# Moving the load of a chunk's shifted rows ahead of a store, the transposes ahead of a layer, and spreading the table gathers 12, 12, 12, 3 instead of 10, 10, 10, 9

## What is computed

```python
e = jnp.stack([tbl_0[ids[:, 0]], ..., tbl_38[ids[:, 38]]], axis=1)      # (2048, 39, 16)
x0 = xk = e
for idx, (W, b) in enumerate([(w0, b0), (w1, b1), (w2, b2)]):
    z = jax.nn.relu(jnp.einsum('bhd,bkd,hks->bsd', x0, xk, W) + b[None, :, None])
    if idx != 2:
        xk = z[:, :64, :]; direct.append(z[:, 64:, :])
    else:
        direct.append(z)
z = jnp.sum(jnp.concatenate(direct, axis=1), axis=-1)                   # (2048, 256)
h = jnp.concatenate([z, dense_ctx], axis=1)
y = relu(relu(h @ W_top1 + b_top1) @ W_top2 + b_top2) @ W_top3
```

## Time and profile before

| | |
|---|---|
| median of 3 runs | 2711.19 us |
| the profiled execution, its own time | 2712.57 us |
| its span, first to last instruction | 2710.9 us |
| mean granted TensorE clock | 0.97 |
| busy: PE, DVE | 2447.7 us (90%), 2228.0 us (82%) |
| busy: ACT, POOL | 1502.6 us (55%), 1610.5 us (59%) |
| DMA | 481.11 MB, mean 177 GB/s |

### The profile page before, as it was taken

The page is one execution under the profiler, slowest core; times in us unless marked ns, Lnnn a source line. Parts: engine busy times, 40 slices in busy tenths (PEclk is TensorE's granted clock), DMA queues, the critical chain, the costliest instruction groups (busy, mean ns, idle before and its releaser), DMA issues.

```text
span 2710.9 us, 27181 instructions
## 1 busy us (share of the span) xinstructions
PE 2447.7 (90%) x7840; PEld 1481.2 (55%) x7840; DVE 2228.0 (82%) x1358; ACT 1502.6 (55%) x1798; POOL 1610.5 (59%) x1093
## 2 busy tenths in 40 slices
PE   0689989898998989999898998989899898989999
PEld 0356555555565555556555555655566555556653
DVE  0679979797998979799798988979789798989970
ACT  0456556565665655556565555655566565556652
POOL 6456657566665756666665666666576566634440
PEclk9899999999999999999999999999999999999999
DMA  2977687777768877776877777787777787787720
GB/s 82 227 184 206 159 195 209 151 201 179 195 168 204 211 146 201 178 181 180 210 188 170 194 176 178 193 203 178 175 199 173 176 205 186 173 186 208 203 67 0
DMA packets 267897, 481.11 MB, mean 177 GB/s; under 512 B 20075, under 2 KB 42715, under 8 KB 267797
## 3 DMA queue, kind: packets, MB, share of 16 engines
q1 hardware_dynamic: 146950, 275.14, 42.0%
q10 hardware_dynamic: 100480, 200.29, 28.3%
q0 software_dynamic: 20448, 5.45, 1.5%
HBM read 470.96 MB, written 9.84 MB: 177 GB/s over the span
## 4 chain that ended last, share of the span: by engine, by line
PE 38%; DVE 18%; issue 17%; DMA 11%; ACT 6%; POOL 4%; SPq 3%; another core or an unknown queue 2%; ACTq 1%; DVEq 0%; POOLq 0%
PE z L796 19%; PE z L775 17%; DVE prod L479 14%; DMA x_diag<-x_transposed 10%; DVE lo_parts L251 3%; ACT hi_parts L610 2%; POOL lo_parts L251 2%; POOL emb L409 1%; ACT hi_copy L624 1%; SPq L300 1%; PE z L897 1%; DVE logit L520 1%; SPq L301 1%; PE xk L897 1%
## 5 line engine op out<-in xcount | busy, mean ns | idle before, releaser
L479 DVE TENSOR_TENSOR prod<-x_pairs,xk 128x2048 f32<-128x2048 f32 x640 | 1432.6, 2280 | 68.5 <-PE z L796 44.7
L251 POOL TENSOR_TENSOR lo_parts<-prod,hi_parts 128x1024 fp32r<-128x1024 f32 x384 | 916.5, 2387 | 759.4 <-ACT hi_parts L610 736.5
L775 PE MATMUL z<-prod,w_plain 128*128 128x512 f32 (+2 forms) x2688 | 1293.0, 604 | 57.8 <-DVE prod L479 35.8
L610 ACT CAST hi_parts<-prod 128x1024 fp32r<-128x1024 f32 x766 | 796.2, 1048 | 832.8 <-DVE prod L479 536.7
L796 PE MATMUL z<-hi_parts,w_lo 128*128 128x512 f32 (+1 forms) x1536 | 858.5, 559 | 145.2 <-DVE lo_parts L251 130.4
L775 PEld LDWEIGHTS z<-prod,w_plain 128*128 128x128 f32 (+2 forms) x2688 | 515.1, 193 | 489.5 <-issue 357.4
L409 POOL DMA_INDIRECT emb<-in_tbl,idx x624 | 603.5, 967 | 255.8 <-issue 175.4
L796 PE MATMUL z<-hi_parts,w_hi 128*128 128x512 f32 (+1 forms) x1536 | 618.2, 402 | 0.0
L796 PE MATMUL z<-lo_parts,w_hi 128*128 128x512 f32 (+1 forms) x1536 | 613.8, 400 | 0.0
L796 PEld LDWEIGHTS z<-hi_parts,w_lo 128*128 128x128 f32 (+1 forms) x1536 | 293.2, 191 | 374.5 <-DVE lo_parts L251 146.4
L479 DVE TENSOR_TENSOR prod<-x_diag,xk 117x2048 f32<-117x2048 f32 (+1 forms) x128 | 256.9, 2007 | 224.4 <-ACT xk L654 155.5
(11 more groups left out here) (69 smaller groups left out, 630.3 us busy)
## 6 DMA issues: line engine op xcount, KB each, us to landing
x_pairs<-x_transposed SPq DMA_DIRECT2D x64, 2432.0 KB
x_pairs<-x_transposed ACTq DMA_DIRECT2D x64, 2432.0 KB
x_diag<-x_transposed SPq DMA_DIRECT2D x128, 546.0 KB
x_diag<-x_transposed ACTq DMA_DIRECT2D x64, 546.0 KB
x_pairs<-x_transposed SPq DMA_DIRECT2D x64, 256.0 KB
emb<-in_tbl,idx POOLq DMA_INDIRECT x624
x_diag<-x_transposed SPq DMA_DIRECT2D x128, 78.0 KB
x_transposed<-stage SPq DMA_DIRECT2D x32, 156.0 KB
```

What stands on the lines that cost most here:

```text
L251: engine.tensor_tensor(lo_parts[0:rows, place:place + m, :], held[0:rows, at:at + m, :], hi, ALU.subtract).then_inc(done, 1)
L479: nc.vector.tensor_tensor(prod[0:rows, pos % RING, 0:n, :], a, xk.unsqueeze(1).broadcast_to([rows, n, N]), ALU.mult).then_inc(prod_ready, 1)
L610: nc.scalar.copy(hi_parts[0:rows, place:place + m, :], held[:, at:at + m, :]).then_inc(hi_ready, 1)
L775: return nc.tensor.matmul(z[n][:], w, held[0:rows, i, :], start=first, stop=last)
```

## The change

Three edits. SP: `load_chunk` gets a parameter `store`, and in chunk 2's turn it issues the two bands of shifted rows of chunk 3 first, then the store of the next group, then chunk 3's `x_pairs`. PE: the eight transposes stand in front of layer 2 of chunk 1, ahead of its wait for `summed2`, instead of inside it. POOL: 24 instead of 20 gathers are issued before the loop, and the chunks 0, 1, 2, 3 issue 12, 3, 12, 12 gathers instead of 10, 9, 10, 10.

```diff
-GATHERS_AHEAD = 20
-GATHERS_AT = [range(20, 30), range(30, F), range(0, 10), range(10, 20)]
+GATHERS_AHEAD = 24
+GATHERS_AT = [range(24, 36), range(36, F), range(0, 12), range(12, 24)]
...
-            def load_chunk(bt, c):
+            def load_chunk(bt, c, store=False):
...
                 for i in range(DIAG - 1):
                     diag_band(sp, chunk, i)
+                if store:
+                    store_group(bt + 1)
...
-                    if c == 2 and not last:
-                        store_group(bt + 1)
                     if c < CHUNKS - 1:
-                        load_chunk(bt, c + 1)
+                        load_chunk(bt, c + 1, c == 2 and not last)
...
-            def layer(n, slot, pos, lows, turn=None, turn_at=None):
+            def layer(n, slot, pos, lows):
...
-                    if k == turn_at:
-                        transpose_group(turn)
...
+                    if c == 1 and not last:
+                        transpose_group(bt + 1)
                     pe.wait_ge(summed2, chunk + 2)
-                    if c == 1 and not last:
-                        layer(2, slot, pos, lows, bt + 1, 1)
-                    else:
-                        layer(2, slot, pos, lows)
+                    layer(2, slot, pos, lows)
```

## The result

The changed kernel takes 2661.01 us (median of 4 runs, 2660.66 to 2665.47) against 2710.55 of the kernel before on the same chip: a ratio of 0.9822 with an interval from 0.9805 to 0.9839, 50 us faster. The forecast was 2578, 133 us faster.

A forecast was written before the change was run, and what follows sets the result against it. PE, busy 90%, was taken as close to the bound, idling for a regular stall on `x_diag`. Windows summed to 150.6 us a group instead of 159.2, 129 us over 15 groups: 2582, leaned to 2578; range 2535 to 2650.

The forecast's parts named there:

- SP's rows in front of the store: SP's chunk 3 rows issue 16.6 us earlier, so the 12.3 us stall in window two goes, with its clock loss.
- no growth of the gathers' losses: Lower bound of the four windows' sum in a loop group: 148.1 us, against 150.6 forecast and 159.2 before.
- the 1.2 us that it charged window three for late releases: PE's releases reach ACT late under gathers; without the stall window three should lose 1.2 us like the others.
- Transposes: On PE, moved in front of chunk 1's layer 2: the same 0.8 us wherever they stand, so cost zero.
- window two: Second of a group's four stretches between PE's layer 2 starts in successive chunks: forecast 36.6 us, transposes included, 48.9 before.
- I take a quarter (0.6 us): Two more gathers in a chunk delay PE's release to ACT by 0.6 us, out of a possible 2.5 us.
- the first rival: Chunk 2's twelve gathers delay releases of layer 1's fifth slot and layer 0; window three 41 to 43 us; chance 0.11.
- The mean clock: Sign of success on PE: the mean granted clock rises from 0.97 to about 1.00.
- POOL's lateness in chunk 2: Twelve gathers make POOL late for layer 2; 1.3 us charged to window three, 1.2 at least, 2.7 at most.
- Gathers take the stall's place: The first rival: saving only 3 to 5 us a group, 2635 to 2665 us in all; chance 0.11.
- The rival of `x_pairs`: Chunk 3's `x_pairs` load becomes late for DVE; if 5 us are missing, 75 come back, 2655 us; chance 0.06.
- The slower case: Late releases grow by more than the gathers' own time in three chunks; at 5 us more each, 2751 us; chance 0.04.

## Why the prediction was wrong

**SP's rows in front of the store: right.** The rows go out 0.16 us behind `sum2`, they land before ACT wants them, DVE's stall and the low clock behind it are gone. SyncE's order alone makes a group 147.8 us; the prediction's sum with no growth of the gathers' losses was 148.1, its lower bound. Of the 1.2 us that it charged window three for late releases, 0.6 were there with ten gathers (36.4 against 35.8).

**Transposes: right**, 0.8 us wherever they stand, but they moved from window two, which is 35.8 us and not 36.6, to window one. At the full clock that one is 37.9 us with them (38.5 in most groups, where it has the low clock of a wait before it), and the prediction had 38.2 without them: it started from 37.6, which is window four's length, and added 0.6 us for two more gathers, but the gathers in window one are chunk 1's, nine before and three now.

**The step that failed: "Whether two more gathers shift the release by their 2.5 us or by nothing, no row shows. I take a quarter (0.6 us)."** In the changed kernel they cost PE most of the 2.5 us. PE stands 2.0 to 2.8 us in front of layer 2 at the end of window three and 2.7 us (the median) at the end of window four; with SyncE's order alone, and nine or ten gathers, PE's whole idle time in a window is 0.6 to 0.8 us (37.00 - 36.41 and 37.30 - 36.50). That is 1.9 us more in window four where 0.6 was forecast, and 2.0 to 2.8 in window three where 1.2 was. It isn't a fixed price: beside the stall the same step from ten to twelve made window four 39.0 us against 37.3 with SyncE's order alone, and window three 37.0 against 36.4.

The reason given for the quarter was that chunks 0 and 3 had ten each and lost different amounts. That says that the loss depends on where the gathers stand, not that more of them cost little. The argument against the first rival, that earlier slots released under gathers had lost little, doesn't carry either: fewer gathers are out at an earlier slot, and releases with at most six out come 0.04 us after PE in these traces. The release isn't tied to the end of the last gather, though it came 1.7 us after it here and 2 us in the earlier trace rows: the gathers held back show 0.04 us with gathers going out for 6 us more.

**What was not counted: the clock behind the new gaps.** The stall's gap had 2.8 us of clock loss beside it, and the prediction counted that as gained. The new gaps bring some back. In the group shown PEclk is 0.96 in both windows (42.9 x 0.04 = 1.7 us, 40.5 x 0.04 = 1.6). It is lost right behind two of the three gaps and not behind the third, as the stretches of 5.8 us from the end of each show (windows of the kernel after):

```profile
1299.30:1305.10 5.80, 5.80 (x16) 3.88 (x17) 2.52 (x2) 2.42 (x4) 5.62 (x3) 0.71 0.04 8
1336.20:1342.00 5.80, 5.79 (x11) 2.64 (x12) 5.80 (x4) 2.90 (x3) 4.52 (x2) 0.71 0.40 72
1376.70:1382.50 5.80, 5.57 (x15) 2.86 (x16) 5.80 (x4) 2.90 (x3) 4.50 (x2) 1.00 0.85 238
```

The first two lose 5.8 x 0.29 = 1.7 us each. Averaged over the loop, the shares of windows one, three and four are 0.970, 0.988 and 0.967, together 3.0 us a group: of the 5.7 us by which a group is longer than forecast (156.3 against 150.6) this is more than half. The mean clock rose from 0.97 to 0.98 and not to 1.00. The Trainium skill (TensorE: Matmul & The Clock Gate, HAM oscillation), which the prediction used for the old gap alone, tells of such losses behind longer idle times than these of 2.39 and 2.69 us; here shorter ones are followed by a low clock too, and the measurement decides. They aren't always: the third gap, the longest with 2.75 us, has 1.00 behind it, and behind a wait of 2.40 us on a chip of the second kind the clock was low in half of the groups and 1.00 in the others. What decides between the two is open. In SyncE's order alone, with no wait of PE in the loop over 1 us, the clock stays at 1.00.

**POOL's lateness in chunk 2: the term was mis-sized**, 1.3 us forecast (1.2 to 2.7), 2.39 measured, near the upper bound. The sum gave each of the twelve gathers 1.26 us, and one took 3.66. On a chip with no late releases it shows alone: 39.3 - 36.8 = 2.5 us in the window and 37 us in all.

Window three by its terms, in the group shown: 35.8 + 2.4 (POOL) + 2.7 (late release) + 1.7 (clock) = 42.6, measured 42.9. Window four: 35.8 + 2.75 + 1.6 = 40.2, measured 40.5. The rival "Gathers take the stall's place" (41 to 43 for window three, 2635 to 2665, given 0.11) has both numbers right, but by luck. Its mechanism was that chunk 2's gathers make chunk 2's own releases late; those came in time (0.04 us, window two is 35.8), and the loss is POOL's lateness, chunk 3's and chunk 0's releases and the clock. The rival of `x_pairs` fell: DVE waits for it once, at the start. The slower case was right in its kind, a growth of the losses in the chunks with twelve, but the growth is 2.9 us in window four (40.5 against 37.6; decisive at 4.1 in all three), and window one, with chunk 1's three gathers, grows only by its clock.

What stays open. The kernel before differs by 3% between the two kinds of chip, and the delay behind the gathers is there on one and not on the other, with the same program. I can't tell the chip itself from something else that changed between the sets, since no chip is known to have run twice; nor what about the gathers delays PE's signal. The kernels meant to test fewer, more or earlier gathers against the delay all fell on chips without it. On both kinds SyncE's order with the old counts is the best version that I found: 0.9406 and 0.9512, with the other places of ten to twelve gathers outside chunk 2 level with it on the second kind. It beats the changed kernel by 4.2% of the kernel before's time on the first kind and by 1.4% on the second.

## What to carry to other kernels

When a change removes a stall, go through what stood in its shadow on every engine, with its own price now: here POOL stood idle for 11.4 us behind chunk 2's gathers before and not at all after. Edits that share such a cover must be timed one by one; the good one alone was worth three times the three together. A term that no row shows (here the shift of a release by more gathers) is better taken near its full size than near nothing, and a new gap in PE's stream is charged with its clock as well, as rows of the kernel before show it for the old gap.

## What the hardware showed unexpectedly

While gathers by index were being issued from POOL (0.94 us busy and one each 1.25 us, some 1.8 to 3.7 us), PE's releases reached ACT up to 3.8 and 4.3 us late on one kind of chip once eight or more had gone out in a chunk, and 0.04 us after PE with six or fewer. The same number of plain loads on the same queue, issued in less than half the time, and as much POOL arithmetic delayed nothing (all windows 35.8 us). In three sets on other chips the releases came within 0.04 us behind as many gathers, in the changed kernel as well. The kernel before took 2694 to 2711 us in three sets and 2628 to 2629 in three others, so a ratio is only worth something against a kernel run beside it.
